# Rows of a routed feed-forward layer sent to expert slots group by group, and read back with plain loads

## What is computed

```python
h = layernorm(x) * (1 + ca) + sa
x = x + ga * attention(h)                      # segments of 128, and a global part
h = layernorm(x) * (1 + cb) + sb               # xf below: 8192 rows of 512
score = softmax(xf @ Wg + bg); gate = max(score); idx = argmax(score)
pos = number of earlier tokens with the same idx
keep = pos < cap                               # cap = 8192 / 16 = 512
buf[idx, pos] += where(keep, xf, 0)            # 16 x 512 x 512
hid = relu(buf @ W1 + b1)                      # W1: 16 x 512 x 2048
y = hid @ W2 + b2                              # W2: 16 x 2048 x 512
out = where(keep, y[idx, pos] * gate, 0)
x = x + gb * out
```

## Time and profile before

| | us |
|---|---|
| median of 3 runs | 1911.46 (1911.04 to 1913.74) |
| the profiled execution | 1909.39 |
| its span, first to last instruction | 1907.7 |
| PE busy | 1821.5 (95%) |
| DVE, POOL, ACT busy | 1226.4, 869.4, 822.3 |
| prologue, until the token loop's first matmuls | about 105 |
| token loop | about 105 to 640 |
| turn to the experts | about 640 to 712.5 |
| expert loop and end | 712.5 to 1907.7 |

### The profile page before, as it was taken

One profiled execution on the slowest core, in us unless ns is written; L12 is line 12 of the kernel. 1 busy time (PEld: TensorE's weight loads), 2 busy tenths in 40 slices (PEclk: granted clock), 3 DMA queues, 4 the chain that ended last, 5 costly groups with the idle time before them and its releaser, 6 DMA issues.

```text
span 1907.7 us, 28124 instructions
## 1 busy us (share of the span) xinstructions
PE 1821.5 (95%) x9137; PEld 1490.8 (78%) x9138; DVE 1226.4 (64%) x1877; ACT 822.3 (43%) x1321; POOL 869.4 (46%) x709
## 2 busy tenths in 40 slices
PE   8999999999999729999999999999998999999998
PEld 3477777778778527889888888888887988888886
DVE  4277888888888745455664544547748887454762
ACT  2445455455455314324443333435545654334541
POOL 2035665666666441244442334335636757233632
PEclk9999999999999969999999999999999999999999
DMA  8034234224224423444534354344545555434622
GB/s 271 29 135 156 89 113 153 89 95 170 88 90 149 162 92 108 144 144 166 178 125 154 127 173 139 122 148 163 185 161 180 191 186 187 170 124 154 214 86 66
DMA packets 137915, 270.77 MB, mean 142 GB/s; under 512 B 17633, under 2 KB 18221, under 8 KB 137862
## 3 DMA queue, kind: packets, MB, share of 16 engines
q1 hardware_dynamic: 115338, 221.27, 33.4%
q0 software_dynamic: 22528, 48.86, 8.0%
HBM read 237.71 MB, written 50.72 MB: 151 GB/s over the span
## 4 chain that ended last, share of the span: by engine, by line
PE 80%; DVE 11%; issue 4%; ACT 2%; POOL 1%; DMA 1%; DVEq 0%; POOLq 0%; ACTq 0%; SPq 0%
PE bank L322 23%; PE bank L324 23%; PE bank L323 23%; PE bank L771 2%; PE bank L707 2%; DVE h L1374 1%; DVE prob L1268 1%; DVE stats L1150 1%; DVE xr L1378 1%; PE bank L814 1%; PE bank L564 1%; PE bank L603 1%; DVE ht_lo L1214 1%; PE bank L532 1%; DVE u_lo L1396 1%
## 5 line engine op out<-in xcount | busy, mean ns | idle before, releaser
L1435 DVE TENSOR_TENSOR h_lo<-h_f,h_hi 128x512 fp32r<-128x512 f32 x256 | 223.5, 894 | 362.7 <-ACT h_f L1087 362.4
L1086 ACT ACTIVATE h_hi<-bank,b_col 128x512 fp32r<-128x512 f32 x256 | 176.7, 690 | 597.6 <-PE bank L324 581.8
L322 PE MATMUL bank<-bt_hi,w_hi 128*128 128x512 f32 (+4 forms) x1024 | 360.5, 352 | 8.4 <-DVE w_lo L1406 6.6
L324 PE MATMUL bank<-bt_hi,w_lo 128*128 128x512 f32 (+4 forms) x1024 | 359.5, 351 | 0.0
L323 PE MATMUL bank<-bt_lo,w_hi 128*128 128x512 f32 (+4 forms) x1024 | 359.3, 351 | 0.0
L322 PE MATMUL bank<-w_hi,h_hi 128*128 128x512 f32 x832 | 326.5, 392 | 2.8 <-DVE h_lo L1435 2.4
L323 PE MATMUL bank<-w_lo,h_hi 128*128 128x512 f32 x832 | 324.9, 390 | 0.0
L324 PE MATMUL bank<-w_hi,h_lo 128*128 128x512 f32 x832 | 324.7, 390 | 0.0
L322 PEld LDWEIGHTS bank<-bt_hi,w_hi 128*128 128x128 f32 x1024 | 194.7, 190 | 34.0 <-issue 9.0
L323 PEld LDWEIGHTS bank<-bt_lo,w_hi 128*128 128x128 f32 x1024 | 194.7, 190 | 20.9
L324 PEld LDWEIGHTS bank<-bt_hi,w_lo 128*128 128x128 f32 x1024 | 194.6, 190 | 20.3
(11 more groups left out here) (252 smaller groups left out, 3264.1 us busy)
## 6 DMA issues: line engine op xcount, KB each, us to landing
raw<-in_L_ffn_W_dram SPq DMA_DIRECT2D x128, 1024.0 KB, 6.9
xa<-in_L_attn_x_dram SPq DMA_DIRECT2D x16, 1024.0 KB, 5.4
xr<-in_L_attn_x_dram SPq DMA_DIRECT2D x16, 1024.0 KB, 7.9
out_dram<-xr SPq DMA_DIRECT2D x16, 1024.0 KB, 9.8
h_rows<-h SPq DMA_DIRECT2D x16, 1024.0 KB, 4.3
b_bc<-in_L_ffn_b_dram SPq DMA_DIRECT2D x16, 256.0 KB, 6.3
wm_b<-in_L_wmod_dram SPq DMA_DIRECT2D x2, 1024.0 KB, 8.2
wm_d<-in_L_wmod_dram SPq DMA_DIRECT2D x2, 1024.0 KB, 5.2
```

The lines of the kernel that those rows point to most:

```text
L322: pe.matmul(o, a_hi, b_hi, start=start, stop=False)
L324: return pe.matmul(o, a_lo, b_hi, start=False, stop=stop)
L1086: act.activation(h1_hi[b % 2][:, j, :], h_bank[j][:, :], ACT.Relu, bias=bias)
L1435: dve.tensor_tensor(h1_lo[b % 2][:, j, :], h1_f[:, j, :], h1_hi[b % 2][:, j, :].bitcast(F32), ALU.subtract) \
```

## The change

The rows of h2 no longer go to DRAM in the order of the tokens to be gathered by a table. Each group's rows are scattered to their slots in a DRAM tensor `slot_dram` (8192 x 512, `slot_rows` in listings) once the group is routed, and an expert's rows are then 512 consecutive rows, loaded by SP.

- The 16 MB of `slot_dram` are cleared by four DMAs of 4 MB from one cleared tile (`no_rows`): two in the prologue, after the load of a modulation weight and before `mod_rows` is written, and one each after SP's first and second iteration.
- SP copies h2 of group i-2 to an on-chip buffer `stage` (1 MB) instead of to DRAM, after the rows of group i-3 have been sent from it. The last two groups are sent from h2 itself.
- POOL's `scatter` becomes `send_rows` (four indirect DMAs of 128 rows of 2 KB) followed by `send_tokens` (the four DMAs of pairs as before). For the last two groups, all rows go first and all pairs after them.
- The gathers of `xh`, the clearing of `xh`, and DVE's copies of token numbers for them are gone; SP loads `xh` with four DMAs of 256 KB per expert.
- At the turn DVE waits until group 15's rows are sent, then does `split_w1` of block 0 and `rows_low(0)`, and waits for the table after these.
- The four buffers of raw weights trade places, since `stage` takes the place of one of them; the load of W2 for block 1 waits until `stage` is free.

The core of the diff, in the order of the file:

```diff
-    h2_dram = nc.dram_tensor("h2_rows", (T, D), F32, kind="Internal").ap()
+    slot_dram = nc.dram_tensor("slot_rows", (E * CAP, D), F32, kind="Internal").ap()
...
+    stage, = over(r_raw0, ("stage", full, F32))
+    no_rows, = over(cursor[0] + 6 * KB, ("no_rows", [P, D], F32))
...
+        def clear_slots(quarter):
+            rows = slot_dram.rearrange("(q p a) d -> q p a d", q=4, p=P)[quarter]
+            sp.dma_start(rows, no_rows[:].unsqueeze(1).to_broadcast([P, E * CAP // P // 4, D])) \
+                .then_inc(slots_cleared, 16)
...
         load_wmod(CB)
+        clear_slots(0)
+        clear_slots(1)
         sp.wait_ge(mod_fixed, 1)
         sp.dma_start(mod_dram[:, VC, :], modr[:, VC, :]).then_inc(vc_stored, 16)
...
-                sp.wait_ge(h2_ready, 4 * g.n + 4)
-                sp.dma_start(group_rows(h2_dram, g), h2[g.par][:]).then_inc(h2_stored[g.par], 16)
+            if prev2:
+                g, before = i.plus(-2), i.plus(-3)
+                if not isinstance(i.n, int) or i.n >= 3:
+                    sp.wait_ge(rows_sent[before.par], 16 * GS * (before.half + 1))
+                sp.wait_ge(h2_ready, 4 * g.n + 4)
+                stand_alone(sp, sp_passed)
+                sp.dma_start(stage[:], h2[g.par][:]).then_inc(h2_staged[g.par], 16)
...
+        def load_xh(e):
+            rows = slot_dram[bass.ds(e * CAP, CAP), :].rearrange("(p j) d -> p j d", j=GS)
+            for j in range(GS - 1, -1, -1):
+                sp.dma_start(xh[:, j, :], rows[:, j, :]).then_inc(xh_in[j], 16)
+        for par in range(2):
+            sp.wait_ge(rows_sent[par], 16 * GS * (NG // 2))
+        load_xh(0)
...
+                if b == 0 and not last:
+                    sp.wait_ge(bt_full, 4 * e + 4)
+                    stand_alone(sp, sp_passed)
+                    load_xh(e + 1)
...
             wait_past(dve, scattered[g.par], 16 * GS * g.half)
+            wait_past(dve, rows_sent[g.par], 16 * GS * g.half)
...
-                    dve.wait_ge(h2_stored[p1.par], 16 * p1.half)
+                    dve.wait_ge(h2_staged[p1.par], 16 * p1.half)
...
-        dve.memset(xh[:], 0.0).then_inc(rows_cleared, 1)
+        dve.wait_ge(rows_sent[(NG - 1) % 2], 16 * GS * (NG // 2))
         split_w1(0, 0, 0)
-
+        rows_low(0)
         dve.wait_ge(table_in, 16)
-        dve.tensor_copy(tok_h[:], tok[:, 0:GS, 0]).then_inc(tok_h_ready, 1)
...
-        rows_low(0)
         dve.memset(xo[:], 0.0).then_inc(rows_cleared, 1)
...
-        def scatter(g):
-
+        def send_rows(g):
+            if isinstance(g.n, int) and g.n == 0:
+                pool.wait_ge(slots_cleared, 16 * 4)
+            late = isinstance(g.n, int) and g.n >= NG - 2
             pool.wait_ge(route, RT * g.n + RT)
+            if late:
+                pool.wait_ge(h2_ready, 4 * g.n + 4)
+            else:
+                pool.wait_ge(h2_staged[g.par], 16 * (g.half + 1))
             stand_alone(pool, pool_passed)
+            for s in range(GS):
+                rows = h2[g.par] if late else stage
+                pool.indirect_dma_start(out=slot_dram, out_offset=bass.IndirectOffsetOnAxis(slot_i[g.par][:, s:s + 1], 0),
+                                        in_=rows[:, s, :], in_offset=None, bounds_check=E * CAP - 1,
+                                        oob_is_err=False).then_inc(rows_sent[g.par], 16)
+        def send_tokens(g):
...
             if prev3:
-                scatter(i.plus(-3))
+                send_rows(i.plus(-3))
+                for k in tokens:
+                    send_tokens(i.plus(k))
...
-        iteration(Group(NG // 2, 1), False, False, True)
-        iteration(Group(NG // 2 + 1, 0), False, False, True)
+        iteration(Group(NG // 2, 1), False, False, True, ())
+        iteration(Group(NG // 2 + 1, 0), False, False, True, (-4, -3))
...
-        with pool.Fori(1, E - 1) as e:
-            gather_h(e + 1)
```

More of the change, by code:

```diff
@@ L209, in build_block @@
     QCS2 = [QC, QCS]
-    raw = over(r_raw0, ("raw0", full, F32)) + over(r_xa, ("raw1", full, F32), ("raw2", full, F32)) \
-        + over(r_ht, ("raw3", full, F32))
+    raw = over(r_xa, ("raw0", full, F32), ("raw1", full, F32)) + over(r_ht, ("raw2", full, F32)) \
+        + over(r_raw0, ("raw3", full, F32))
     w1_hi, w1_lo, w2_hi, w2_lo = [None] * 2, [None] * 2, [None] * 2, [None] * 2
@@ L279, in build_block @@
     x2_stored = [sem(f"x2_stored{i}") for i in range(2)]
-    h2_stored = [sem(f"h2_stored{i}") for i in range(2)]
+    h2_staged = [sem(f"h2_staged{i}") for i in range(2)]
     h2t_full, h2t_done, parts_full, parts_out, lg_full = (sem(k) for k in (
@@ L285, in build_block @@
     scattered = [sem(f"scattered{i}") for i in range(2)]
+    rows_sent = [sem(f"rows_sent{i}") for i in range(2)]
     count_full, rows_counted = sem("count_full"), sem("rows_counted")
-    table_in, index_step, tok_h_ready, tok_x_ready, gate_ready, gb_in, gb_gated = (sem(k) for k in (
-        "table_in", "index_step", "tok_h_ready", "tok_x_ready", "gate_ready", "gb_in", "gb_gated"))
+    table_in, index_step, tok_x_ready, gate_ready, gb_in, gb_gated = (sem(k) for k in (
+        "table_in", "index_step", "tok_x_ready", "gate_ready", "gb_in", "gb_gated"))
     w1_in = [sem(f"w1_in{i}") for i in range(2)]
@@ L428, in _, with iteration @@
         sp.dma_start(sb_tab[:], spread(SB, P)).then_inc(late_tab_in, 16)
-        def iteration(i, cur, prev, load2):
+        def iteration(i, cur, prev, prev2, load2):
             if load2:
@@ L448, in iteration @@
                 sp.dma_start(group_rows(out_rows, g), xr[g.par][:]).then_inc(x2_stored[g.par], 16)
+            if prev2:
+                g, before = i.plus(-2), i.plus(-3)
+                if not isinstance(i.n, int) or i.n >= 3:
+                    sp.wait_ge(rows_sent[before.par], 16 * GS * (before.half + 1))
                 sp.wait_ge(h2_ready, 4 * g.n + 4)
-                sp.dma_start(group_rows(h2_dram, g), h2[g.par][:]).then_inc(h2_stored[g.par], 16)
-        iteration(Group(0, 0), True, False, True)
-        iteration(Group(0, 1), True, True, True)
-        with sp.Fori(1, NG // 2 - 1) as half:
+                stand_alone(sp, sp_passed)
+                sp.dma_start(stage[:], h2[g.par][:]).then_inc(h2_staged[g.par], 16)
+        iteration(Group(0, 0), True, False, False, True)
+        clear_slots(2)
+        iteration(Group(0, 1), True, True, False, True)
+        clear_slots(3)
+        iteration(Group(1, 0), True, True, True, True)
+        iteration(Group(1, 1), True, True, True, True)
+        with sp.Fori(2, NG // 2 - 1) as half:
             for par in range(2):
-                iteration(Group(half, par), True, True, True)
+                iteration(Group(half, par), True, True, True, True)
         for n in range(NG - 2, NG):
-            iteration(Group(n // 2, n % 2), True, True, False)
+            iteration(Group(n // 2, n % 2), True, True, True, False)
         def load_w1(n, par):
@@ L1489, in expert @@
                 n = NB * e + b
-                if b == 0 and not last:
-                    for j in range(GS):
-                        dve.wait_ge(xh_in[j], 16 * (e + 1))
-                    stand_alone(dve, dve_passed)
-                    dve.tensor_copy(tok_h[:], tok[:, bass.ds(GS * (e + 1), GS), 0]).then_inc(tok_h_ready, 1)
                 split_hidden(e, b, 0)
@@ L1589, in scatter, with iteration @@
                                         oob_is_err=False).then_inc(scattered[g.par], 16)
-        def iteration(i, prev, nxt, prev3):
+        def iteration(i, prev, nxt, prev3, tokens=(-3,)):
             p1 = i.plus(-1)
```

22 lines of the change are left out of this document (7 added, 15 removed).

## The result

| | us |
|---|---|
| before, median of 4 runs | 1912.24 (1911.04 to 1913.74) |
| changed, median of 4 runs | 1939.11 (1937.10 to 1939.72) |
| ratio | 1.0137, 95% interval 1.0122 to 1.0152 |
| span of the profiled execution | 1935.3 (before 1907.7) |

The change costs 26.9 us by the medians and 27.6 us by the two profiled executions. To see where, I read the start of the same piece of work in both traces; the last column is how far the changed kernel is behind at that point. One execution each of two kernels further down (the one with both edits, 3088.56 us, and the one with DVE's clearings moved, 2330.20 us) ran at a much lower granted clock (0.56 and 0.75 instead of 0.98) and is left out of their medians.

The account below looks back on a forecast made before the run. PE was taken to bound both loops, other engines counting only where PE waits. Loop 19, turn 3, prologue 0 and expert loop 0 gave 22 on 1909.4: 1931.4 profiled, 1933 at the median, range 1912 to 1948 for 8 in 10.

Parts of the forecast that it names:

- A send costs 1.30 us whatever it carries: POOL's token-loop queue: each indirect DMA takes 1.30 us regardless of bytes, so four more per iteration are 5.2 us.
- Rival 4: Token loop: DVE's longer two-input work holds up POOL's extra sends, 17 us more, 1949; chance 0.07.
- The root is 2.0 to 2.5 us late: Token loop: POOL's extra sends outlast its idle before the inverse root, so ACT's waiting instructions begin 2.0 to 2.5 us late.
- PE's stall by iteration: Token loop, iterations 3 to 14: PE waits 1.0, 1.7 or 2.3 us for DVE's `ht_lo`, 19 us over twelve.
- iteration A: First of three token-loop iterations examined: ACT 2.0 us late, slack 1.0 before PE needs `ht_lo`, so PE waits 1.0.
- Iterations 15 and 16: Iterations at the turn, also carrying the sends with little slack: 2.7 and about 1.6 us late, 4.4 in all.
- The turn: Token loop to expert loop: `hidden` of expert 0 earlier, but late table delays block 1; net +3 us, from -2 to +7.
- The clock: At the turn: PE's idle gap of some 7 us before block 1 lowers the granted clock, priced at 2 us.
- Prologue: Two clears ahead of the `mod_rows` store make `g_b` 8.4 us late, covered by DVE's 13.82 us of idle: 0.
- The rival of slow clears: Prologue, SP's queue: clears at 200 GB/s take 42 us and exceed DVE's cover, +13, so 1946; chance 0.08.
- Rival 1: Token loop: slack takes the sends, since DVE's statistics may still release the root; 1909 to 1915; chance 0.11.
- Rival 2: Loop absorbs the sends and the turn keeps its 6 us, with the table landed before about 711: 1905; chance 0.08.

Follow-up runs that it names:

- both edits: Changed kernel with row sends placed after POOL's modulation of h2 and DVE's table wait, indices and clearings moved behind block 1's split_w1: 1912.56 us, ratio to before 1.0009.
- the run with four: Changed kernel with all four clears of slot_dram in the prologue, instead of two there and two in the first iterations: 1949.66 us.
- the run with the divided sends and moved table work: Changed kernel with four row and two pair sends ahead of the root, two pairs behind h2's modulation, DVE's table work behind block 1's split_w1: 1902.46 us.

## Why the prediction held, step by step

Forecast 1933 (1912 to 1948), measured 1939.1: the direction and the cause were right, the size 27 instead of 22.

- **A send costs 1.30 us whatever it carries.** Right: rows 0.97 to 1.06 us with 0.30 between them, and the run with four extra pairs shows the same loss as rows do. Rival 4, DVE holding the sends in the loop, is out: the longest row send there took 1.42, and only the first of an iteration was that long. At the turn two pair sends, at 721.66 and 723.88 beside DVE's cast and subtraction of 2048 columns, took 1.91 and 2.03.
- **The root is 2.0 to 2.5 us late.** Right: it begins 1.9 to 2.6 us behind DVE's statistics in every iteration with both, 2.0 in the one shown, where before it was 0.1.
- **PE's stall by iteration.** The sum was right (19 forecast, 19.4 by its own terms, 19.6 measured), its parts were not, so the closeness of the sum is partly luck. I let iteration A use a slack of 1.0 us each time and had the stall grow from 1.0 to 2.3. The trace has a period of 37.7 us from the third iteration on, after its first two within 0.2 us, and 36.0 before, so every iteration pays about the same 1.7: a slack can be spent once, in the first iterations, and what counts after that is the length of the closed chain from the sends over ACT and DVE to PE and back to DVE's `pay`, for which the next sends wait. The stall also showed in two places. The wait for `ht_lo` is 0.73 us an iteration, under the 1 to 2.3 that I had named as its sign; the rest is `u_lo`, which came later too (0.9 to 1.5 us of wait instead of 0.4 to 1.1).
- **Iterations 15 and 16.** 4.4 forecast, 4.9 measured.
- **The turn.** The shape was right, its terms were not. The first `hidden` was forecast 6 us earlier than the loop's delay would put it, and is 2.6 earlier (17.4 behind, where the loop is 20.0 behind). By the last token counts it gained 7.4, but by that measure the forecast had over 10: 6 on top of the 4.4 of iterations 15 and 16. From the end of the row sends (720.07) to `hidden` it took 9.9 us, not 8. The sends themselves ended late too: in all eight traces of kernels built on the change POOL stands idle for 2.0 to 2.1 us between the first and the second of them, and the profile names no releaser. The gap of about 7 us before block 1 was 6.46, so block 1 comes 4.0 later than the loop's delay puts it, where I had 1.0 to 1.4. The clock cost less than I had. The table by stretches shows it granted at 0.50, the lower of the two levels (1.2 GHz), in 748 to 752 with PE busy all the time, after PE had stood nearly still from 741 to 747.5; block 1 took 13.3 us of PE, where block 0 had taken 11.2. But behind the next wait (2.58) it stayed at 1.00, where before it fell to 0.52, and 1.6 us came back: 0.7 net, where I had 2. Together the turn with its two iterations cost 4.8 where the forecast had 3: block 1 came 2.8 later than I had it, and the clock cost 1.3 less.
- **Prologue.** Right: SP's reads of `g_b` moved by 21.6 us (62.19 instead of 40.57) where I had 22, DVE used `g_b` at 67.14 against 68, and nothing was left of it at the work behind. The rival of slow clears is out, and the run with four shows where it would have begun.
- **The end.** The term that was missing: 2.1 us behind the last scatter. It is the largest part of the 5.6 us by which the sum fell short of the profiled execution; the turn has 1.8, the second half of the expert loop 0.7, the loop 0.6 and its start 0.4. I had it at nothing without looking, and no run shows what makes it.
- **Rival 1**, slack that takes the sends, failed at its own words: `ht_lo` had nothing to regain. **Rival 2**, the table landing in time, named the gain that the run with the divided sends and moved table work then had, though not by an earlier table: there DVE only comes to it later.

The Trainium skill, "DMA: Bandwidth & Descriptors", section "Anatomy of one DMA — SWDGE (gpsimd) path", gives a DMA of this kind about 2.0 us fixed plus its bytes at 436 GB/s. By that, as an estimate, a send of pairs lands after 2.0 and one of 256 KB after 2.6. The trace agrees for these two, with 2.1 and 2.7 us median to landing; the gathers of before, with the same 256 KB, took 3.7. Nothing above is worked out from it: what cost time here was the issue of each send on POOL, not its landing.

## What to carry to other kernels

Count what an in-order engine issues ahead of the value that others wait for, and compare the sum with its idle time just there, not with its busy share: POOL was 59% busy in this loop, yet it had room for two more sends at that place and not for four: four cost 24 us, while four behind its other work cost 3. When an order is changed so that something arrives early, look at what now stands behind it in each queue: here the pairs, and with them the table that DVE waits for in order. And a design that loses may have its gain hidden under a bad order; the idea of this change is worth an estimated 3 to 5 us once the sends and DVE's table work are placed by what waits for them.

## What the runs showed of the hardware

- An indirect DMA of 128 rows cost POOL the same with 8 bytes a row as with 2 KB: 0.97 to 1.06 us and 0.30 us between two; the first of a group took up to 1.5 in the loops of all these kernels.
- Clearing DRAM from one tile of 2 KB a partition went as fast as other writes or faster: the table by stretches shows 410 GB/s between 44 and 52 us of the changed kernel, against 379 in the microsecond of the h2 store. The two clears added in the run with four moved `g_b` by 21.9 us, which is 383 GB/s.
- Executions of one kernel differ by up to 7 us. Part of it is whether the clock falls after an idle stretch. In the prologue the sixteen transposes of xa took 1.97 us in one trace and 3.63 in that of the kernel with both edits, whose prologue is the same. PE had been idle just as long ahead of them, 1.97 and 1.96 us; the granted clock was 1.00 from 108 to 114 in the first, and 0.50 from 110 to 112 in the second:

```profile
108.07 1.97 PE L637 MATMUL bank<-ident,xa 128*128 128x128 f32 x16 [1.97 <-POOL xa L1594]
```

```profile
109.06 3.63 PE L637 MATMUL bank<-ident,xa 128*128 128x128 f32 x16 [1.96 <-POOL xa L1598]
```

- The time from the last scatter to the end of the span was 6.1 to 6.2 us in all six traces of kernels built on before and 8.4 in all eight of kernels built on the change, though the last instructions are the same.
